# First routed sequence: the last local probabilities turned before the null products, the null logits moved before the expanded queries on VectorE

## The reference, cut to what matters

```python
local_out = local_mha(x, ...)                 # 16 heads, windows of 64 tokens, each sees itself and the window before
q_idx, q_scores, queries, _ = router(xw, rt_q, qmask, NQ)           # 32 of each window's 64 tokens, for 2 groups
_, kv_scores, key_values, kv_mask = router(ctx, rt_kv, ctx_mask, NKV)   # up to 128 of the tokens before the window
# grouped attention: per group g, 16 heads, one learned null key and value beside the chosen ones
sim = concat([q @ null_k, q @ k.T]) * DIM_HEAD ** -0.5
o   = softmax(sim) @ concat([null_v, v])
out = (local_out + scatter(o)) / counts
```

## Time and profile before

| | us |
|---|---|
| median of 3 runs | 778.88 |
| lowest, highest | 778.61, 780.72 |
| the profiled execution | 778.74 |
| its span | 776.9 |
| TensorE busy | 731.4 (94%) |
| VectorE busy | 477.9 (62%) |
| ScalarE busy | 420.9 (54%) |
| GpSimd busy | 225.2 (29%) |

### The profile page before, as it was taken

One profiled execution on the slowest core, in us unless ns is written; L12 is line 12 of the kernel. 1 busy time (PEld: TensorE's weight loads), 2 busy tenths in 40 slices (PEclk: granted clock), 3 DMA queues, 4 the chain that ended last, 5 costly groups with the idle time before them and its releaser, 6 DMA issues.

```text
span 776.9 us, 17339 instructions
## 1 busy us (share of the span) xinstructions
PE 731.4 (94%) x6062; PEld 562.4 (72%) x6068; DVE 477.9 (62%) x1076; ACT 420.9 (54%) x1527; POOL 225.2 (29%) x309
## 2 busy tenths in 40 slices
PE   4999999999999899999999999789999999999996
PEld 3778788878886566666666667668778787787875
DVE  5433333369886787777777764575665656656563
ACT  3344444432224567667776774475665756657462
POOL 3130000000003797776677741021312211001011
PEclk9999999999999999999999998999999999999997
DMA  8601000000001323333333330000000000000001
GB/s 250 285 1 56 0 0 0 0 0 0 2 0 43 91 60 81 88 83 86 84 83 85 85 86 1 1 12 8 17 4 14 10 8 2 0 0 0 0 1 55
DMA packets 26063, 32.69 MB, mean 42 GB/s; under 512 B 7056, under 2 KB 15760, under 8 KB 25360
## 3 DMA queue, kind: packets, MB, share of 16 engines
q1 hardware_dynamic: 24720, 29.25, 13.6%
q0 software_dynamic: 1280, 2.62, 1.3%
HBM read 12.98 MB, written 2.10 MB: 19 GB/s over the span
## 4 chain that ended last, share of the span: by engine, by line
PE 57%; DVE 10%; issue 9%; POOL 8%; ACT 6%; POOLq 6%; DVEq 2%; DMA 1%; SPq 1%; ACTq 0%
PE ps L735 9%; PE ps L747 9%; PE ps L999 7%; PE ps L1059 6%; POOLq L570 4%; PE ps L1026 4%; PE ps L722 4%; PE ps L1042 4%; PE ps L716 4%; ACT stage L1282 3%; POOL early L562 3%; DVE stage L1622 2%; PE ps L1035 2%; POOL early L581 2%; POOLq L572 2%
## 5 line engine op out<-in xcount | busy, mean ns | idle before, releaser
L562 POOL TENSOR_TENSOR early<-stage 128x512 f32<-128x512 f32 x64 | 89.0, 1412 | 55.6 <-DVE stage L1622 38.5
L1282 ACT ACTIVATE stage<-ps,nmB 128x128 f32<-128x128 f32 x256 | 90.2, 381 | 22.3 <-DVE nmB L1655 21.8
L1338 ACT ACTIVATE early<-ps,nmC 128x128 f32<-128x128 f32 (+1 forms) x224 | 77.7, 363 | 43.4 <-DVE dnC L1718 43.3
L747 PE MATMUL ps<-stage 128*128 128x128 f32 (+2 forms) x448 | 86.1, 321 | 1.4 <-DVE stage L1520 1.2
L735 PE MATMUL ps<-stage,early 128*128 128x128 f32 (+2 forms) x448 | 86.4, 321 | 0.0
L735 PEld LDWEIGHTS ps<-stage,early 128*128 128x128 f32 x448 | 65.2, 191 | 24.5 <-issue 15.5
L747 PEld LDWEIGHTS ps<-stage 128*128 128x128 f32 x448 | 65.5, 191 | 12.1 <-issue 1.9
L1026 PEld LDWEIGHTS ps<-stage,early 128*128 128x128 f32 x448 | 55.5, 191 | 25.5 <-issue 25.5
L1227 ACT ACTIVATE stage<-ps 128x512 f32<-128x512 f32 x64 | 31.4, 491 | 65.2 <-PE ps L735 65.2
L1042 PE MATMUL ps<-early,stage 128*128 128x512 f32 (+1 forms) x112 | 59.2, 610 | 4.3 <-ACT early L1350 4.3
L1026 PE MATMUL ps<-stage,early 128*128 128x128 f32 (+1 forms) x448 | 60.0, 280 | 3.3 <-DVE early L1691 2.5
(11 more groups left out here) (196 smaller groups left out, 1495.1 us busy)
## 6 DMA issues: line engine op xcount, KB each, us to landing
early<-early SPq DMA_DIRECT2D x256, 64.0 KB, 2.0
x<-in_x SPq DMA_DIRECT2D x4, 256.0 KB, 4.4
stage<-in_cq SPq DMA_DIRECT2D x1, 1024.0 KB, 7.2
stage<-in_ck SPq DMA_DIRECT2D x1, 1024.0 KB, 9.1
stage<-in_cv SPq DMA_DIRECT2D x1, 1024.0 KB, 11.1
stage<-in_co SPq DMA_DIRECT2D x1, 1024.0 KB, 13.1
early<-in_wqk SPq DMA_DIRECT2D x1, 1024.0 KB, 14.3
xrows<-xhat SPq DMA_DIRECT2D x1, 1024.0 KB, 5.2
```

The costliest lines, as they stand in the source:

```text
L562: pool.tensor_tensor(to, a, b, (ALU.subtract, ALU.add)[f]).then_inc(rot_in, 1)
L747: t = pe.matmul(ps[:, b, q0:q1], vN[:, b % 2, m, :], simA[:, b % 2, s, at:at + q1 - q0], start=False, stop=False, skip_group_check=True)
L1282: t = act.activation(pB[:, u % 2, at, :], ps[:, 4 + h, i * P:(i + 1) * P], ACT.Exp, bias=nmB[:, u % 2, at:at + 1], accum_out=rsB[:, u % 2, ...
L1338: act.activation(pC[:, k, hg, 0:n], ps[:, 5 + k, hg * P:hg * P + n], ACT.Exp, bias=nmC[:, k, hg:hg + 1], accum_out=rsC[:, k, hg:hg + 1])
```

## The change

Three blocks move, all in the first sequence and nothing else; no instruction is added or removed.

```diff
@@ TensorE, sequence
                 if not before:
+                    b_turn_probs(end)
                     pe.wait_ge(qsel_in, B)
                     nulls()
                 expand(g, b, it, 0)
                 expand(g, b, it, 1)
                 if before:
                     turn_probs(pit, 5)
-                else:
-                    b_turn_probs(end)
                 turn(it, 0)
@@ ScalarE, sequence
                 if before:
                     mixed(before[2], 3)
-                expanded(g, it, 0)
                 if not before:
                     b_probs(end)
+                expanded(g, it, 0)
                 turned(it, 0)
@@ VectorE, sequence
             def sequence(g, b, it, before):
+                if not before:
+                    null_logits()
                 expanded(g, it, 1)
...
                 expanded(g, it, 5)
-                if not before:
-                    null_logits()
                 expanded(g, it, 7)
```

## The result

The changed kernel takes 773.22 us (median of 7 runs, 772.78 to 774.42), the kernel before in the same rounds 778.61 (775.35 to 780.82): a ratio of 0.9936, 95% interval 0.9915 to 0.9957. Two repeats gave 0.9934 (0.9909 to 0.9958) and 0.9938 (0.9924 to 0.9953). The interval of this one ratio (3.3 to 6.6 us) still holds the 3.4; over all timed runs of both kernels, in the table further down, the means differ by 4.8 us (standard error 0.32), which does not.

What follows compares the result with a forecast made beforehand. TensorE, busy 94% of the span, was taken to bound the kernel, with its waits and half clock in the first sequence. 0.92 + 2.49 = 3.41 us off 778.74 gave 775.3, range 773.8 to 776.9.

Steps and rivals of the forecast that it cites:

- part one and two: First sequence: transposes moved ahead of the null products gain 0.92 us; null logits ahead of VectorE's first share gain 2.49.
- Part two's limit: VectorE's first expanded share ends 0.08 us before expansion 3 needs it, cost 0; next limit: null products' end plus 4.4 us.
- rival 2: VectorE becomes the limit, null logits hold up expansion 3: 776.7 at far end, about 776.3 in the middle; chance 0.14.
- I keep the fall where it is: At the null products: clock still falls to half at 481.42 us and rises about 488.24; no clock term in the sum.
- A gap of 2.49 us between wide work left the clock full: Idle time ahead of the first scores: no clock fall there, which spoke for the end without any fall, 773.9.
- the one case of no fall at the null products: Clock stays full through null products and expansions: gain 4.8 us, time 773.9; chance 0.17.
- the chances of "same" and "slower": Whole kernel: within about 0.3% (2.3 us) of no change, chance 0.15; slower than that, 0.03.
- Rival 4: Clock falls a second time among the first scores: 0.59 per us at half clock, 6.8 us giving 779.3; chance 0.04.
- Rival 3: Gap before the first scores is taken by the local result's copy or the exponentials: 777.8; chance 0.05.

Runs made afterwards that it cites:

- its form filled ahead of the scores: Kernel before with two wide products, result unused, put in TensorE's idle time just ahead of the first scores; 1.0012 of the kernel before.
- the halves: Kernel before with only the transposes and their evacuations moved, 0.9974 of the kernel before; with only the null logits moved, 0.9951.
- the nine other kernels: All timed kernels except the kernel before: the changed one and the edited forms; together their runs give 0.29 us for each us at half clock.
- the hole put back: Changed kernel with seven memsets on VectorE between its third and fourth share, restoring idle time ahead of the first scores; 779.03 us, 1.0012 of the kernel before.
- the spread kernel: Changed kernel with null products in four parts behind expansions 0 to 3, null logits behind VectorE's second and third shares; 770.48 and 770.22 us.

## Why the prediction was wrong

- **The places, part one and two: right.** Forecast 0.92 and 2.49, together 3.41; measured 0.96, 2.4 to 2.5, and together 3.2 to 3.4 in profiles with alike first half clock (18.45 and 18.27 against 21.66 in the kernel before and 21.67 in its form filled ahead of the scores), 2.8 with a short one (17.19 against 19.96 and 20.04; the wait for VectorE, 0.31 us, comes off the gain there). The fit over all runs gives 3.15 (standard error 0.26) together, but 1.6 and 2.1 (0.3 each) for the halves; the profiles are the closer reading.
- **Part two's limit: right.** The first share starts 0.09 us after the null logits, and TensorE waits for it only where the clock rises early, 0.31 us (rival 2, in one of three profiles).
- **The step that failed: "I keep the fall where it is".** The clock stood in the sum as zero, because the half clock of one execution was taken for that of the kernel. It differs from run to run, and its mean goes from 13.6 to 9.0 us with the change: 4.6 us at 0.357, or 1.6 us (1.3 at the price of the nine other kernels). 3.15 and 1.63 add up to the 4.8 us by which the means differ, as they must in such a fit. In the profiled pair alone the clock helped only at the end of the program, so that pair does not show this step; the runs do. How the 4.6 us divide between the null products, the first scores and the end is open, with two profiles of the kernel before and three of the changed one. The step's reason was off as well: it counted 0.9 us of transposes in the last 3 us before the fall, where its own times (second half 478.3 to 478.85, fall at 481.42) give 0.4.
- **The row that misled.** "A gap of 2.49 us between wide work left the clock full" is true of that execution. With the hole put back, half clock grows by 5 us over 12 runs; in the other profile of the unchanged kernel it came a second time just there, as in four of the five profiles with that gap. The gap was counted for its idle time alone.
- **The range.** Its lower end, 773.8, was the one case of no fall at the null products, made against an execution that also lost 1.1 us to half clock at the end. Second falls and the end of the program were in no bound of it, so it was too high for the middle of the measured runs. (A slip without effect: by its own terms the chances of "same" and "slower" add up to 0.16 and 0.02, not 0.15 and 0.03.)
- **The rivals.** Rival 4's mechanism was there, in the profiled execution itself (0.92 us for 3.4 at half clock, 0.27 each where it reckoned 0.59), but a stretch at half clock there came more often where the gap was open (four profiles of five), so it turns to the change's favour. Rival 3 did not come: exponentials follow the first scores by 2.04 us, before 2.05.
- **The Trainium skill's rule** that the monitor of the clock is not reset by a kernel ("TensorE: Matmul & The Clock Gate", Part 1) agrees with the runs: in the five profiles of the kernel before and the changed kernel the first fall lies between about 478.7 and 482.6 us, 0.4 to 3.3 us after the start of the null products. It was used for a spread around zero; it should have been used to ask which of the two kernels leaves more stretches in which a fall can come.

## What to carry to other kernels

A change that closes an idle time of TensorE is worth the idle time and what that idle time does to the clock; one profiled execution shows one throw of the latter, so read the mean granted clock of all runs of the kernel before, and give the range its spread. Ask also where the half clock lies: here a us of it cost about 0.5 at the null products and expansions, where TensorE was busy without a pause, 0.2 to 0.3 among the first scores, where it also waits, and nothing behind the last product. Here the clock fell after idle time and a run of narrow products, and did not in two profiles once the same products alternated with wide ones; that kernel took 3 us less than the changed one. Where an idle time can't be closed, wide products with an unused result in it may still pay: here they did with both gaps filled (six runs), and not clearly with one.

## What the runs showed that was not expected

- The kernel before spreads over 8.4 us (774.12 to 782.51 in 87 runs), the spread kernel over 3.4 (769.33 to 772.75 in 11). The half clock of the former's runs goes from 4.6 to 20.3 us, which at 0.357 is 5.6 of the 8.4.
- Dummy work made the unchanged kernel 0.4 to 0.8% faster (0.9941, 0.9922 to 0.9960, six runs).
- The local stage, which the change doesn't touch, varied between 235.0 and 237.3 us from its first product to the last pick over these profiles; why was not tried.
